# A graph network's second layer: GpSimd's gathers written out, with their row numbers read in place

## What is computed

```python
def _typed_pass(feat, W, bias, src_idx, dst_idx, etypes, norm_per_edge, n):
    proj = jnp.einsum('ni,rio->rno', feat, W)      # 16 relations
    m = proj[etypes, src_idx] + bias
    m = m * norm_per_edge[:, None]
    return segment_sum(m, dst_idx, num_segments=n)
m_forward = _typed_pass(feat, Wf, forward_bias, src, dst, etypes, norm_f, n)
m_backward = _typed_pass(feat, Wb, backward_bias, dst, src, etypes, norm_b, n)
return s + m_forward + m_backward
```

## Time and profile before

| | us |
|---|---|
| median of 3 runs | 4249.81 |
| the profiled execution's own time | 4253.87 |
| its span, first to last instruction | 4251.8 |
| busy: TensorE 3419.2, VectorE 2448.4, GpSimd 2875.8, ScalarE 984.1 | |
| mean granted TensorE clock | 0.897 |

### The profile page before, as it was taken

How to read it: one execution, slowest core, us unless ns; L and a number is a source line. 1 busy time by engine, 2 the same in 40 slices (tenths; PEclk the granted TensorE clock), 3 DMA queues, 4 the chain that set the end, 5 groups by cost and what they waited for, 6 DMA issues and landing times. The chain is left out here.

```text
span 4251.8 us, 76376 instructions
## 1 busy us (share of the span) xinstructions
PE 3419.2 (80%) x21136; PEld 2903.1 (68%) x21137; DVE 2448.4 (58%) x3368; ACT 984.1 (23%) x1538; POOL 2875.8 (68%) x4645
## 2 busy tenths in 40 slices
PE   6999999999999979966766677677567677777776
PEld 5999898989999868755555555565445556565555
DVE  6888888888888888835555522222423333333333
ACT  3454444544444444400011011110100000000000
POOL 2777777777777500077777777777587777777773
PEclk8999999999999989978888888888878789888888
DMA  5555555555555436634444464444333223233332
GB/s 168 170 169 165 168 168 166 169 163 169 166 164 164 141 124 206 206 111 137 130 138 136 128 140 142 129 136 134 100 91 89 84 85 89 84 88 89 89 89 83
DMA packets 322748, 569.93 MB, mean 134 GB/s; under 512 B 73896, under 2 KB 218392, under 8 KB 322584
## 3 DMA queue, kind: packets, MB, share of 16 engines
q0 software_dynamic: 137984, 411.19, 34.1%
q1 hardware_dynamic: 182732, 154.33, 11.3%
q10 hardware_dynamic: 1868, 2.52, 0.2%
HBM read 452.43 MB, written 115.41 MB: 134 GB/s over the span
## 5 line engine op out<-in xcount | busy, mean ns | idle before, releaser
L436 POOL DMA_INDIRECT fa<-ptab,slot x784 | 819.0, 1045 | 338.8 <-issue 187.1
L491 POOL DMA_INDIRECT hr<-proj,gslot x784 | 761.7, 972 | 280.5 <-issue 145.4
L476 POOL DMA_INDIRECT fa<-proj,gslot x400 | 393.3, 983 | 381.1 <-issue 295.3
L722 PE MATMUL pc<-ws,hr 128*128 128x256 f32 x4704 | 611.0, 285 | 4.7 <-issue 3.5
L722 PEld LDWEIGHTS pc<-ws,hr 128*128 128x128 f32 x4704 | 573.7, 189 | 11.0 <-issue 10.2
L732 PE MATMUL pa<-fa,onehot 128*128 128x256 f32 x904 | 264.0, 445 | 207.2 <-DVE onehot L1054 112.3
L732 PEld LDWEIGHTS pa<-fa,onehot 128*128 128x128 f32 x904 | 196.4, 223 | 260.2 <-issue 204.1
L774 PE MATMUL pu<-hr,fa 128*128 128x258 f32 x1056 | 289.4, 416 | 102.8 <-issue 100.7
L1087 DVE TENSOR_TENSOR acc<-acc,pa 128x256 f32 x196 | 82.2, 419 | 496.5 <-remote 331.8
L774 PEld LDWEIGHTS pu<-hr,fa 128*128 128x128 f32 x1056 | 218.1, 208 | 162.8 <-issue 129.3
L774 PE MATMUL pa<-hr,fa 128*128 128x258 f32 x1040 | 282.8, 418 | 56.7 <-issue 54.8
(11 more groups left out here) (166 smaller groups left out, 6077.9 us busy)
## 6 DMA issues: line engine op xcount, KB each, us to landing
proj<-fa SPq DMA_DIRECT2D x400, 256.0 KB
fa<-in_ea_t SPq DMA_DIRECT2D x196, 128.0 KB
fa<-ptab,slot POOLq DMA_INDIRECT x784
hr<-proj,gslot POOLq DMA_INDIRECT x784
fa<-in_Wrel SPq DMA_DIRECT2D x32, 256.0 KB
ptab<-fa SPq DMA_DIRECT2D x25, 256.0 KB, 2.0
fa<-proj,gslot POOLq DMA_INDIRECT x400
ws<-proj,gslot POOLq DMA_INDIRECT x192
```

Of the source, the lines that this page charges most:

```text
L436: pool.indirect_dma_start(pbuf[:, n % 2, j, :], None, ptab[:, :], bass.IndirectOffsetOnAxis(ap=slot[:, n, j:j + 1], axis=0)).then_inc(s_ga ...
L476: pool.indirect_dma_start(gbuf[n][:, j, :], None, proj[0][:, :], bass.IndirectOffsetOnAxis(ap=gslot[:, at, j:j + 1], axis=0)).then_inc(s_g ...
L491: pool.indirect_dma_start(raw2[:, n, j, 0:H], None, proj[1][:, :], bass.IndirectOffsetOnAxis(ap=gslot2[:, n, j:j + 1], axis=0)).then_inc(s ...
L722: last = nc.tensor.matmul(pc[:, j, :], uT[:, par, a, j // 2, kk, j % 2 * P:(j % 2 + 1) * P], w2s[:, c, kk, :], start=False, stop=(j == jj ...
```

## The change

- In both gather stages of the second layer GpSimd's program is written out: a plain loop at build time over 196 supertiles, 784 gathers in a row per stage, with no branch.
- Each gather takes its 128 row numbers from its own column of `row_src` or `row_dst`.
- `gslot`, `gslot2`, the 1504 copies of one column, the two copies that filled the buffers first (L462, L482), `s_rows`, `s_rows2`, the waits on them, the waits of copies on `s_gath[2]` and the increments of `s_go` in these stages are gone.
- The waits on `s_agg`, `s_pst`, `s_sb` and `s_self` stay; so do the numbers of buffers, the first layer's gathers and every instruction of the other engines.

```diff
--- before.py
+++ after.py
@@ -105,8 +105,6 @@
         tops = sb("tops", [P, 8 * S2])
         win = [sb(f"win{k}", [1, ST], I32) for k in range(2)]
         slot = sb("slot", [P, GS, J], I32)
-        gslot = sb("gslot", [P, 2 * RF, J], I32)
-        gslot2 = sb("gslot2", [P, RS, J], I32)
         onehot = sb("onehot", [P, 3, J, P])
 
         fa = sb("fa", [P, 10240])
@@ -208,7 +206,6 @@
         s_in1 = sem("s_in1")
         s_out2 = sem("s_out2")
         s_plan = sem("s_plan")
-        s_rows = sem("s_rows")
         s_gath = [[sem(f"s_gath{k}_{h}") for h in range((2, RF, RS)[k])] for k in range(3)]
         s_back = sem("s_back")
         s_ea = [sem(f"s_ea{k}") for k in range(2)]
@@ -227,7 +224,6 @@
         s_xoh = [sem(f"s_xoh{k}") for k in range(3)]
         s_xadd = [sem(f"s_xadd{k}") for k in range(3)]
         s_ones = sem("s_ones")
-        s_rows2 = sem("s_rows2")
         s_xagg = [sem(f"s_xagg{k}") for k in range(3)]
         s_self = sem("s_self")
         s_sb = sem("s_sb")
@@ -294,32 +290,6 @@
                 for n in range(GS):
                     yield GS * i + n, n, i
 
-
-        def sixteens(eng):
-
-            def sixteen(i):
-                for m in range(2 * RF):
-                    yield 2 * RF * i + GS + m, (GS + m) % RF, 2 * i + (GS + m) // RF, (GS + m) % (2 * RF)
-
-            for n in range(GS):
-                yield n, n, 0, n
-            yield from sixteen(0)
-            with eng.Fori(1, (ST - GS) // (2 * RF) - 1) as i:
-                yield from sixteen(i)
-            yield from sixteen((ST - GS) // (2 * RF) - 1)
-
-        def twelves(eng):
-
-            def twelve(i):
-                for m in range(RS):
-                    yield RS * i + GS + m, (GS + m) % RS, i + (GS + m) // RS
-
-            for n in range(GS):
-                yield n, n, 0
-            yield from twelve(0)
-            with eng.Fori(1, (ST - GS) // RS - 1) as i:
-                yield from twelve(i)
-            yield from twelve((ST - GS) // RS - 1)
 
         @block.sync
         def _(sp):
@@ -450,51 +420,28 @@
             for n in range(GS):
                 gather_nodes(ST - GS + n, n)
             pool.wait_ge(s_zero[0], 1)
-            def copy_index(slots, at, j, rows, s, done):
-                s = s if isinstance(s, int) else pool.snap(nc.s_assert_within(s, 0, ST - 1, skip_runtime_bounds_check_because="the last are left out"))
-                last = nc.gpsimd.tensor_copy(slots[:, at, j:j + 1], rows[:, bass.ds(J * s + j, 1)])
-                if j == J - 1:
-                    last.then_inc(done, 1)
-
-            def ends(s, ahead):
-                return isinstance(s, int) and s + ahead >= ST
-
-            nc.gpsimd.tensor_copy(gslot[:, 0:RF, :].rearrange("p a j -> p (a j)"), row_src[:, 0:RF * J]).then_inc(s_rows, 1)
+            def gather_rows(buffer, table, rows, s, landed):
+                for j in range(J):
+                    pool.indirect_dma_start(buffer[:, j, 0:H], None, table,
+                                            bass.IndirectOffsetOnAxis(ap=rows[:, J * s + j:J * s + j + 1], axis=0)
+                                            ).then_inc(landed, 16)
+
             for n in range(5):
                 pool.wait_ge(s_pst[n], 16 * 5 * (NQ // 2))
             pool.wait_ge(s_sb, 1)
-            for s, n, rnd, at in sixteens(pool):
-                if past(s, RF):
+            for s in range(ST):
+                if s >= RF:
                     pool.wait_ge(s_agg[1], s - RF + 2)
-                    pool.wait_ge(s_rows, s - RF + 2)
-                else:
-                    pool.wait_ge(s_rows, 1)
-                    if s == RF - 1:
-                        pool.wait_ge(s_self, NB)
-                pool.sem_inc(s_go, 1)
-                for j in range(J):
-                    pool.indirect_dma_start(gbuf[n][:, j, :], None, proj[0][:, :],
-                                            bass.IndirectOffsetOnAxis(ap=gslot[:, at, j:j + 1], axis=0)
-                                            ).then_inc(s_gath[1][n], 16)
-                    if not ends(s, RF):
-                        copy_index(gslot, (at + RF) % (2 * RF), j, row_src, s + RF, s_rows)
+                if s == RF - 1:
+                    pool.wait_ge(s_self, NB)
+                gather_rows(gbuf[s % RF], proj[0][:, :], row_src, s, s_gath[1][s % RF])
             reduce_windows(1)
-            nc.gpsimd.tensor_copy(gslot2[:, 0:RS - GS, :].rearrange("p a j -> p (a j)"), row_dst[:, 0:(RS - GS) * J]).then_inc(s_rows2, 1)
             for n in range(5):
                 pool.wait_ge(s_pst[n], 16 * 5 * NQ)
-            for s, n, rnd in twelves(pool):
-                if past(s, RS):
+            for s in range(ST):
+                if s >= RS:
                     pool.wait_ge(s_agg[2], s - RS + 2)
-                pool.wait_ge(s_rows2, s - RS + GS + 2 if past(s, RS - GS) else 1)
-                pool.sem_inc(s_go, 1)
-                for j in range(J):
-                    pool.indirect_dma_start(raw2[:, n, j, 0:H], None, proj[1][:, :],
-                                            bass.IndirectOffsetOnAxis(ap=gslot2[:, n, j:j + 1], axis=0)
-                                            ).then_inc(s_gath[2][n], 16)
-                    if not ends(s, RS - GS):
-                        if j == 0 and past(s, GS):
-                            pool.wait_ge(s_gath[2][(n - GS) % RS], 16 * J * (rnd + 1 if n >= GS else rnd))
-                        copy_index(gslot2, (n - GS) % RS, j, row_dst, s + RS - GS, s_rows2)
+                gather_rows(raw2[:, s % RS, :, :], proj[1][:, :], row_dst, s, s_gath[2][s % RS])
 
 
         @block.scalar
```

## The result

| | before | after |
|---|---|---|
| median, us | 4252.27 (4249.64 to 4257.58) | 4226.75 (4217.56 to 4228.6) |
| the profiled execution's own time | 4253.87 | 4227.82 |
| forward stage, first to last gather | 1203.6 | 1187.4 |
| backward stage, first to last gather | 1166.7 | 1149.0 |
| rounds (forward, backward) | 55, 47 | 70, 67 |

The ratio is 0.993, with an interval of 0.9911 to 0.995. Both medians are of four runs. A round is the stretch from one pause of GpSimd to the next; a pause is a gap of over 2.5 us from the start of the gather before to that of a supertile's first gather, once the stage's first supertiles are out. A stage with 55 rounds so has 56 pauses.

The account below looks back on a forecast made before the run. No engine is full; GpSimd gathers in rounds and pauses for TensorE's held-up counts. 17 + 4 = 21 us off the profiled 4253.87 gives 4233; the median, 4.06 lower, was forecast at 4229, range 4185 to 4272.

Parts of the forecast that it names:

- 17 us from denser gathers: Both gather stages: without copies, 345 supertiles in regular rounds save 0.05 us each; ends 0 and 113 us.
- 4 us from the opening: Start of the backward stage: 52 gathers come sooner, so the first pause and TensorE's release come 4 us sooner.
- the increments of `s_go`: Both gather stages: removing them was to give nothing, as the buffer wait and the stores cover them.
- The rounds save 0.06 us per supertile by the pairs shown: Last rounds of both stages: paired with and without copies, they showed 0.06 us saved per supertile; 0.05 was taken.
- The loops: GpSimd's gather loops in both stages: a return costs nothing by the trace, so writing them out gives nothing.
- my 24 us: Loop returns of both stages: by the skill's fetch rule, 24 fewer would make the sum 24 us better; not adopted.
- my 1.0 us per fetch: Instruction fetches: 68 us of packets / 67 on the instruction queue's row, used to price returns and longer code.
- The index in place: Gathers of both stages: reading row numbers from the wide tensor gives nothing; bounds nothing and 0.02 us.
- GpSimd's issue is the bound: First of four rivals, both stages: pauses keep their length and 113 us are gained, giving 4137; chance 0.10.
- Shorter rounds: Rival, both stages: denser gathers bring pauses earlier; at 2 supertiles per round 50 us slower, 4300; chance 0.21.
- Pauses of 2.0 to 2.9 us: Sign in the profile after: GpSimd pauses staying this long would prove that its issue is the bound.
- Rounds of 3 in the backward stage: Sign in the profile after: backward rounds of 2 and 3 supertiles would prove the rival that foresaw a slower kernel.

Follow-up runs that it names:

- set 3: Third set of runs, on K1: the changed kernel and three variants, against the kernel before at 4311.68 us.
- marker_back: The changed kernel with the increments of `s_go` put back ahead of each supertile's gathers: 4301.73 us, ratio 0.9984.
- written_out: The kernel before with only its two gather loops written out, copies and increments of `s_go` kept: 4290.02 us, ratio 0.9947.
- before_again: The kernel before, unchanged, run again on K2 with its own profile: 3865.09 us, ratio 0.9999.
- K1: Kind of chip on which the unchanged kernel takes 4252 to 4312 us; that the chip makes the difference is not shown.
- K2: Kind of chip, met in one set of runs alone, on which the unchanged kernel takes 3866 us and the changed one 3754.71.

## Why the prediction was right, and where not

**The time: right by luck, the terms wrong.** My sum had 17 us from denser gathers, 4 us from the opening, and for "the increments of `s_go`" the word "Nothing, since the buffer wait and the stores cover them". That step failed. The increment does not stand beside the wait but behind it, between the count's arrival and the gather, and nothing covers it: it adds 0.54 to 0.63 us to each of some 100 to 140 releases. What that is worth in the end depends on what else is there. Put back alone it takes 35.7 of the 44 us that the change gives in set 3 (4311.68 to 4267.25). Taken out behind the loops and ahead of the copies it gives 18.1, where the loops had given 19.3. On the first chip the whole change gave 25.5, and no run divides that. I had seen the place: GpSimd 0.60 us behind VectorE. I read it as "released with VectorE" and did not ask what lay between.

**"The rounds save 0.06 us per supertile by the pairs shown": true of a round, not of the stage.** Rounds of 3 take 18.0 us in marker_back and 18.2 in written_out, of 4 supertiles 23.5 and 23.9. But without copies rounds are shorter and more, 121 in place of 102, and this kernel is 11.7 us slower. With the quick release, the copies' removal gives nothing measurable (0.9906 and 0.9898). The 17 us were not there. The pairs I used were few and stood at the end of the stage, and could not show the size of the rounds to come.

**The opening: nothing of the 4.** I took the first pause to stand behind 52 gathers again. It stood behind 48 and was longer, 6.62 us in place of 4.47, and at the 53rd gather the stage was 2.1 us behind the kernel before.

**The loops: open.** Priced at nothing; alone they gave 0.9947 on one chip. By the Trainium skill, "Runtime: NRT & Kernel Launch", section "Instruction fetch mechanics", a taken branch forces a fetch if its target is out of the window, and my 24 us by it come near the 23 measured. Nothing else bears it out. The looped backward stage fetched no packet of instructions in 940 us (in the forward one other engines' packets hide GpSimd's), and neither loop of before_again shows a stall at a return, where no pause could hide it. So this trace does not contradict the page, as I had written: with nothing fetched, the rule gives these returns no cost. Two of my readings were wrong besides. The row at 4128.97 opens supertile 183, the last of the last turn. Supertile 172, whose first gather stands behind a return, starts 44 gathers earlier, and as I said, as any other:

```profile
4065.48 0.97 POOL L491 DMA_INDIRECT hr<-proj,gslot  x1 [0.15 <-issue]
```

And my 1.0 us per fetch came from a queue that GpSimd's code does not change: q8 moves 67 packets in before, written_out and after alike, q14 97, 117 and 103. For the 8 fetches that I allowed for the longer code the changed kernel has 6 packets more.

**The index in place: right.** 0.95 us from the wide tensor as from the small buffer.

**"GpSimd's issue is the bound", 113 us, chance 0.10: false on K1, exact on K2.** 1504 x 0.075 = 113, measured 111. Whether this rival holds differs from one set of runs to another, and one profile could not tell me so.

**"Shorter rounds": the mechanism came, the price did not.** The backward stage now runs rounds of 3 supertiles. I priced a round at 5.7 us per supertile and 0.8 once, and put the turn at a mean of 3.0 supertiles. The mean is 392 / 137 = 2.9, past that point, and the kernel is faster: the medians of after, 11.7 us for 2 supertiles and 17.4 for 3, give 5.7 per supertile and 0.3 once. The release had been most of the 0.8. With the increment back the copies' removal does cost time, 11.7 us (4290.02 to 4301.73), as this rival had it.

**Two of my signs misled.** Pauses of 2.0 to 2.9 us were to prove the first rival. They are 2.6 where the release is 0.56 us quicker and 3.6 to 3.8 with the increment back, and that rival is false on this chip. Rounds of 3 in the backward stage were to prove the slower one. Both signs took the cost of a release for a constant.

## What to carry to other kernels

Where an engine pauses for a count, put the wait on the very instruction that goes on. One increment in between added 0.56 us to each release, and on the chips with pauses it was worth 18 to 36 us of the 44. Ask first whether anyone needs it: in this kernel no engine waits for `s_go`. Where one does, the increment could stand ahead of the wait or behind the gathers; that was not tried. Compare the engines that one event releases; the one that comes later has something in its way. A cheaper issue helps only where the issue is the bound, and that may differ from one chip, or one occasion, to the next: the same text was 0.9% faster on one chip and 2.8% on another, and two idle copies per gather were the fastest version on the first (0.9853) and 4.6% slower on the second.

## What the runs showed of the hardware

- **Two kinds of chip, or of occasion.** One text takes 3866 us in one set of runs and 4252, 4309 and 4312 in the three others. In the backward stage TensorE is granted 0.99 there, and 0.81 to 0.85 in the others.
- **TensorE's counts are held up on K1 alone.** With gathers 1.25 or 1.33 us apart they come late and free GpSimd mostly in rounds of 2 to 5 supertiles; at 1.44 us GpSimd's waits sum to 89 us in place of 396, though VectorE waits as long. What holds them up stays open: neither the bytes of a gather nor the number of buffers was tried on such a chip.
- **A release costs 0.26 us or 0.80 to 0.89**, from count to gather, without and with an increment between.
- **GpSimd's loop of 12 supertiles fetched nothing.** In 940 us of turns the backward stage of before moved no packet of instructions, the same gathers written out 11 with copies (written_out) and 5 without (after, 3190 to 4110 us).
- **Two copies in a row overlap on GpSimd**, by the profile, whose spans on this engine are rough: they take 0.19 and 0.17 us and start 0.13 apart. The step is firm: the second adds 0.11 us to it (1.33 to 1.44).
